# Memory attention on one Trainium2 core: reciprocal row sums as exp(-log) on ScalarE, and value tables cleared after the row normalisation

## The reference

```python
q = _ln((x @ Wq + bq).reshape(b, s1, H, HD), qn_w, qn_b)          # H = 16 heads of HD = 16
k, v         = (main part of the memory, 112 rows of 128)          # k normalised by _ln
k_dca, v_dca = (last 16 rows of the memory, own weights)           # k_dca normalised by _ln
def _attn(q, k, v):
    s = jnp.einsum('bhqd,bhkd->bhqk', q, k) * SCALE
    return jnp.einsum('bhqk,bhkd->bhqd', jax.nn.softmax(s, axis=-1), v)
ctx = _attn(qT, k, v) + _attn(qT, k_dca, v_dca)
x = x + (ctx @ Wo + bo)
```

## Time and profile before

| | |
|---|---|
| median of three runs | 2103.78 us |
| profiled execution, whole | 2098.66 us |
| its span (first to last instruction) | 2096.9 us |
| PE busy | 1824.5 us (87%) |
| DVE busy | 1308.0 us (62%) |
| ACT busy | 967.0 us (46%) |
| POOL busy | 511.2 us (24%) |
| mean granted TensorE clock | 0.952 |

### The profile page before, as it was taken

The page is one execution under the profiler, slowest core; times in us unless marked ns, Lnnn a source line. Parts: engine busy times, 40 slices in busy tenths (PEclk is TensorE's granted clock), DMA queues, the critical chain, the costliest instruction groups (busy, mean ns, idle before and its releaser), DMA issues. The chain is left out here.

```text
span 2096.9 us, 39399 instructions
## 1 busy us (share of the span) xinstructions
PE 1824.5 (87%) x14930; PEld 1475.0 (70%) x14930; DVE 1308.0 (62%) x2415; ACT 967.0 (46%) x1939; POOL 511.2 (24%) x557
## 2 busy tenths in 40 slices
PE   7877757899999899998676786999999997999898
PEld 4756624579998688887255674677777776888666
DVE  4575586755655744444665756788888885666632
ACT  2343475255556322223124324666676663455532
POOL 1020010033332535350120012444555442000200
PEclk9999977999999999999887997999999999999999
DMA  2020000021000201100000010000111102111000
GB/s 92 3 83 3 3 27 16 7 78 31 23 23 23 91 31 41 50 0 28 12 13 1 3 39 8 24 27 27 30 30 30 30 23 98 39 30 38 1 1 21
DMA packets 13503, 61.50 MB, mean 29 GB/s; under 512 B 1872, under 2 KB 2000, under 8 KB 11216
## 3 DMA queue, kind: packets, MB, share of 16 engines
q1 hardware_dynamic: 13392, 59.95, 8.4%
HBM read 58.90 MB, written 1.05 MB: 29 GB/s over the span
## 5 line engine op out<-in xcount | busy, mean ns | idle before, releaser
L2377 DVE SCALAR_TENSOR_TENSOR arena<-bank,arena 128x508 f32<-128x508 f32 (+2 forms) x204 | 151.7, 744 | 35.1 <-ACT arena L2373 23.0
L2502 PE MATMUL bank<-L3a_wo,L3a_y_gated 128*128 128x256 f32 x512 | 124.0, 386 | 0.0
L2708 DVE TENSOR_TENSOR L3a_decays<-L3a_decays,L3a_cb_masked 128x512 f32<-128x512 f32 x128 | 94.7, 802 | 43.8 <-ACT L3a_decays L2593 43.8
L2525 PE MATMUL bank<-L3a_xnT_high,L3a_w_high 128*128 128x512 f32 x256 | 106.6, 416 | 10.6 <-POOL L3a_w_low L2828 9.1
L2593 ACT ACTIVATE L3a_decays<-bank 128x512 f32<-128x512 f32 x128 | 66.1, 603 | 99.3 <-PE bank L2476 99.3
L2502 PEld LDWEIGHTS bank<-L3a_wo,L3a_y_gated 128*128 128x128 f32 x512 | 92.4, 190 | 17.6 <-issue 7.3
L1867 ACT ACTIVATE L1f_silu<-bank 128x512 f32<-128x512 f32 x64 | 38.3, 599 | 141.2 <-PE bank L1833 141.2
L1833 PE MATMUL bank<-L1f_xnT_high,L1f_high 128*128 128x512 f32 x256 | 100.4, 392 | 2.7 <-DVE L1f_hidden L1896 2.7
L2525 PE MATMUL bank<-L3a_xnT_high,L3a_w_low 128*128 128x512 f32 x256 | 100.4, 392 | 0.0
L2525 PE MATMUL bank<-L3a_xnT_low,L3a_w_high 128*128 128x512 f32 x256 | 100.2, 391 | 0.0
L1833 PE MATMUL bank<-L1f_xnT_low,L1f_high 128*128 128x512 f32 x256 | 99.8, 390 | 0.0
(11 more groups left out here) (575 smaller groups left out, 5280.7 us busy)
## 6 DMA issues: line engine op xcount, KB each, us to landing
arena<-in_L3p SPq DMA_DIRECT2D x32, 388.0 KB, 3.0
arena<-in_L1f SPq DMA_DIRECT2D x8, 1536.0 KB, 6.8
arena<-in_L1x SPq DMA_DIRECT2D x18, 384.0 KB, 3.0
arena<-in_L3x SPq DMA_DIRECT2D x18, 384.0 KB, 3.1
arena<-in_L0f SPq DMA_DIRECT2D x1, 4224.0 KB, 13.6
arena<-in_L3f SPq DMA_DIRECT2D x1, 4055.0 KB, 13.1
arena<-in_L2x SPq DMA_DIRECT2D x1, 1989.0 KB, 8.4
arena<-in_L0a SPq DMA_DIRECT2D x1, 1571.0 KB, 10.0
```

The lines of the kernel that those rows point to most:

```text
L2377: return nc.vector.scalar_tensor_tensor(dst[:, :, d:], psum[:, :, 0:P - d], wcol, dst[:, :, d:], ALU.mult, ALU.add)
L2502: mm = nc.tensor.matmul(ps[g // 2][:, (g % 2) * C:(g % 2 + 1) * C], yg[:, o, g * P:(g + 1) * P], wo[:, o, :], start=False, stop=False, ski ...
L2525: mm = nc.tensor.matmul(bank(name, half)[:, :], wm[a][:, kc, :], (xh, xl)[b][:, kc, half * HALF:(half + 1) * HALF], start=(kc + at == 0), ...
L2708: nc.vector.tensor_tensor(d, d, cbm[:, 4 * half:4 * half + 4, :].rearrange("p b t -> p (b t)"), ALU.mult).then_inc(S["dec_ready"], 1)
```

## The change

Three edits. In stages with `M = 2` the row sums leave their bank as logarithms (line 508: `Ln` in place of `Copy`), a new ScalarE step `invert` makes exp(-log) of them in place, behind the four exponents of the pass, and VectorE's reciprocal is left out: its multiplication reads the result of `invert`. The table of ScalarE is preloaded as the set that has both functions. And `ln.read(pool)` moves ahead of `clear`.

```diff
@@ SmallHeads.copy_out, M == 2
-            self.nc.scalar.activation(od[:, 1, :], self.bank(s, 1)[:, :], ACT.Copy).then_inc(self.s_oread, 1)
+            self.nc.scalar.activation(od[:, 1, :], self.bank(s, 1)[:, :], ACT.Ln).then_inc(self.s_oread, 1)
+
+    def invert(self, act, s):
+
+        od = self.od[:, s % 2, :, :]
+        act.wait_ge(self.s_oread, s + 1)
+        self.nc.scalar.activation(od[:, 1, :], od[:, 1, :], ACT.Exp, scale=-1.0).then_inc(self.s_rec, 1)
 
     def act(self, act):
-        self.nc.scalar.preload_act_table(ACT.Exp)
+        if self.M == 1:
+            self.nc.scalar.preload_act_table(ACT.Exp)
+        else:
+            self.nc.scalar.preload_act_table_set("natural_log_exp_and_others")
         for s in range(self.NS + 1):
             if s < self.NS:
                 self.copy_max(act, s)
@@
             if s < self.NS:
                 self.exponent(act, s)
+            if s and self.M == 2:
+                self.invert(act, s - 1)
@@ SmallHeads.normalise
-        nc.vector.reciprocal(self.rec[:, :], od[:, 1, :]).then_inc(self.s_rec, 1)
+        if self.M == 1:
+            nc.vector.reciprocal(self.rec[:, :], od[:, 1, :]).then_inc(self.s_rec, 1)
         dve.wait_ge(self.s_rec, s + 1)
@@
-            nc.vector.tensor_tensor(od[:, 0, :], od[:, 0, :], self.rec[:, :], ALU.mult).then_inc(self.s_op, 1)
+            nc.vector.tensor_tensor(od[:, 0, :], od[:, 0, :], od[:, 1, :], ALU.mult).then_inc(self.s_op, 1)
@@ l2_xattn, gpsimd
+                ln.read(pool)
                 clear(nc, a.v[:, :, :, :, :, :], a.s_zero)
                 pool.wait_ge(s_w, 16)
-                ln.read(pool)
                 add_bias(nc, x, w["bo"], s_bias)
```

## The result

The changed kernel has a median of 2091.26 us (2088.32 to 2093.8, 5 runs) against 2103.78 (2101.16 to 2108.26, 5 runs): ratio 0.9938, interval 0.9921 to 0.9954. A second comparison of the same two kernels gave 0.9959 (0.9946 to 0.9973), so the size itself needs an explanation, and the stages come first.

The account below looks back on a forecast made before the run. It took memsets to bound the stage's head and a chain through three engines, none full, to bound each pass. 6.56 + 0.9 + 0.72 = 8.2 us off the 2103.78 us median gave 2095.6 us, range 2091.8 to 2100.0.

Parts of the forecast that it names:

- The head, 6.56 us: Start of the stage: with `ln.read` ahead of `clear`, memsets can't hold the normalisation; 6.56 us gained, bounds 4.5 and 6.6.
- the 0.9 to 1.5 I had allowed: Projection loop: VectorE's small scaling of the means (line 2178) may be held until the memsets end, 0.9 to 1.5 us.
- The copy of v: Projection loop: the first copy of v waits for `s_zero`, 0.6 to 1.2 us late, absorbed by slack.
- The passes, 0.9 us: Six passes: each goes from 8.90 to 8.75 us, as `invert` is queued behind the exponents; 0.9 us, bounds 0 and 1.5.
- The end, 0.72 us: After the last values: the last addition ends sooner, but TensorE is busy with the first three projections; 0.72 us gained.
- the 1.5 us for the spread of the runs: Whole kernel: allowance of 1.5 us for run-to-run spread, within the range's lower end of 2091.8 us.
- the table loads: Rival, inside each pass: a table load at every change between `Ln` and `Exp`, 5.8 us slower, 2109.6 us; chance 0.04.
- The estimate that stands beside their price: Passes: a table switch of 2.66 us with its drain in place of 1.283 would put that case at about twice the loss.
- The reciprocal's full return: Rival, passes: the removed reciprocal's time comes back in full, 26.8 us, giving 2070 us; chance 0.02.
- The port hold: Rival: the hold by memsets moves into the projection loop, the head keeps about 2 us, time 2100.2 us; chance 0.10.
- The dip of the clock in the last pass: Last pass: dip lost or doubled is 1.7 us either way; rival, reaching the projections, up to 3.5 us, 2099, chance 0.08.

Follow-up runs that it names:

- the run with the reciprocal beside: The changed kernel with a VectorE reciprocal of the same size, into a tile nobody reads, where VectorE would wait for `invert`: 2096.25 us, stage 143.45 us.
- the wait alone: The kernel before, with GpSimd waiting until its own four steps on the memory are finished before it starts the 16 memsets: 2091.17 us, stage 143.81 us.

## Why the prediction was right, and where it was wrong

**The head, 6.56 us: right.** Measured 15.13 - 8.57 = 6.56. Nothing was left over in the projection loop; the small scaling was held 0.22 us, far less than the 0.9 to 1.5 I had allowed, and the addition of the bias and the reduction (lines 2186 and 2189 after) took their 0.69 us each beside the memsets, unheld. The copy of v waited for `s_zero`, as said, and nobody waited for it. By the Trainium skill, SBUF — State Buffer, section "SBUF: two separate sides", a step with two SBUF inputs is held only by a GpSimd step that reads SBUF, so not by a memset. The trace agrees: the centring of block 0 took 0.69 us beside the memsets, and that of block 1 took 1.07 beside the bias. The hold "for the whole instruction" that the Trainium skill states there is enough for the small scaling, but not for the kernel before, where one instruction of VectorE waited for some thirteen of GpSimd.

**The passes, 0.9 us: the mechanism right, the size a third to a half.** Measured from the first scores to the first projection it is 78.30 us before and 77.82 after, 0.48. Of this the six passes of the sum gave 0.33, and the rest lies in the first pass, which differs by as much between profiles of one kernel (10.23 and 10.00 us before). `invert` ends where I put it (0.65 us in place of 0.63), but VectorE starts its multiplication 0.14 us behind it, not 0.03: I took the latency from another pair of instructions, the copy of the row sums and the reciprocal. With VectorE busy until 0.15 us after the end of `invert`, in the run with the reciprocal beside, the multiplication followed at once and the pass was 8.75 us, my figure.

**The end, 0.72 us: right.** 9.26 us from the first projection to the next stage before, 8.54 after.

**Not foreseen: 0.85 us between the head and the passes.** The second group of transposes (line 2123 before, 2135 after) takes less. The granted clock was 0.50 over the whole of it before, and 0.66 in the changed kernel (0.94 from 1117 to 1119, then 0.50 again):

```profile
1123.55 3.68 PE L2123 MATMUL bank<-const,arena 128*128 128x128 f32 x16 [2.99 <-ACT L2x_km L2161]
```

```profile
1117.82 2.83 PE L2135 MATMUL bank<-const,arena 128*128 128x128 f32 x16 [2.99 <-ACT L2x_km L2173]
```

It didn't repeat as a fixed sum: the group took 3.19 us in the second profile of the changed kernel and 2.91 with the head's edit alone (stage 142.85), but 3.68 with the wait alone (stage 143.81), whose head is as short. So the stage gave 6.56 + 0.85 + 0.48 + 0.72 = 8.61 us, against the 8.2 of the sum. That these are so close is in part luck: 0.85 that wasn't foreseen stands against 0.4 too much for the passes.

**The step that failed is the last one: from the stage to the median, and with it the lower end of the range.** The mechanism and the stage's sum held; the term that was too small is the 1.5 us for the spread of the runs, read from three runs of the kernel before. In its place the first comparison put 3.9 us between the stage's 8.6 and the medians' 12.5. The kernel's 27 runs in one comparison spread over 10.9 us, and a median of five carries part of that into the result. The second comparison gave 9.3 us. The intervals of their ratios overlap from 0.9946 to 0.9954, and the stage's 8.61 us is 0.9959, inside the second and outside the first.

Where the spread comes from can be read in the 14 profiles. The seven stages ahead of the changed one do the same work in all of them, and took from 1057.0 to 1067.3 us together. Among the 27 runs of the kernel before, those with a mean granted clock of 0.946 or 0.947 took 2105.7 to 2108.4 us, those with 0.951 or 0.952 took 2097.6 to 2103.9. The first five runs of the changed kernel had 0.951 to 0.953. So the spread goes with the clock; no run sets the clock, and which is the cause isn't shown.

Theory B, a gain for good in later stages, isn't supported by the profiles. The four stages behind the changed one took 876.5 us in the first profile of the changed kernel, after 879.1, but 879.5 in the second. Over all profiles they took 879.0 us on average in the six profiles with the new passes and 879.3 in the eight others, between 876.5 and 881.1. Yet the first comparison and that of `invert` ahead of the exponents both lie above their stage's gain by more than their intervals allow, the second of them narrowly, and none lies below by as much. What made these kernels faster than their stages explain, by some 3 to 4 us, stays open.

The rivals: the table loads didn't come (one load, 1.28 us, at line 520 before the passes). The estimate that stands beside their price was wrong twice. By the rival's own steps, the 2.66 us for a switch, which is from the Trainium skill, ScalarE: Activation LUTs, section "What ACT_TABLE_LOAD costs", would make it 4.5 us a pass in place of 1.75 (an estimate), and not about twice the loss. And the trace of the kernel before doesn't bear out the drain: at 1271.06 a load of 1.28 us starts 0.02 us after one ScalarE step and the next starts 0.01 us after the load. The reciprocal's full return didn't come either, and where the exponents no longer stand before `invert` it isn't 3.35 us a pass but 0.87. The port hold didn't move into the loop. The dip of the clock in the last pass was neither lost nor longer: its values took 5.3 us before and after, and the projections ran at 1.00.

## What to carry to other kernels

Work taken off an engine is worth only what ends later than everything that stands beside it: here 3.35 us came down to 0.05 a pass, because the step that replaced it was queued behind the very work that had hidden most of it; put into the gap ahead of that work it is worth 0.87 us a pass (8.90 to 8.03). When one step takes fifteen times its usual length, look at the other engine's instructions beside it and at what precedes them: a wait can be enough to let it through. And take the width of a range from the spread of the whole program in many runs, not from the stage that changed.

## What the runs showed that was not expected

- A train of GpSimd memsets right behind its own copies held a VectorE step on SBUF data until the train ended (6.23, 6.35 and 6.65 us with 16, 2.48 us with 8); the same train behind a wait, or as the first thing of the stage, let it through in 0.73 and 0.44 us, and ran 8.09 us in place of 7.53.
- VectorE started 0.14 us after the end of `invert` when it had waited for it, and 0.07 us after it when it came from the reciprocal put back (1163.71 against 1163.64). The length of its idle time doesn't explain this: after 1.71 us and after 4.76 us of waiting for the copy of the row sums it started 0.03 us behind that.
- A reciprocal of 128x512 on VectorE costs 3.35 us; a logarithm and an exponential of the same size on ScalarE 0.60 and 0.65.
- The same kernel's first stage took 107.7 us at a granted clock of 1.00 throughout and 112.2 in a run where it was 0.83 from 40 to 60 us and again from 100 to 110.
